# Sixteen small matmul tiles or thirty-two: the numerator product of a linear attention, cut by 32 channels in place of 64

## The reference

```
q, k, v = split(relu(x @ Wqkv.T))                     # 16 x 512 x 32 heads x 8
vk      = sum over tokens of [v, 1] (outer) k         # per head 9 x 8
num     = vk @ q                                      # per token and head 9 numbers
att     = num[:8] / (num[8] + 1e-15)
x       = layernorm(x + att @ Wp.T + bias)
h       = silu(x @ Wg.T) * (x @ Wu.T)                 # 768 hidden channels, weights int32 / 127
out     = layernorm(x + h @ Wd.T)
```

## Time and profile before

| | |
|---|---|
| median of three runs | 493.71 us |
| the profiled execution's own time | 493.46 us |
| its span, first to last instruction | 491.5 us |
| mean granted TensorE clock | 0.999 |
| TensorE matmuls busy | 485.7 us (99%) |
| VectorE busy | 417.6 us (85%) |
| ScalarE busy | 231.7 us (47%) |
| GpSimd busy | 87.5 us (18%) |

### The profile page before, as it was taken

How to read it: one execution, slowest core, us unless ns; L and a number is a source line. 1 busy time by engine, 2 the same in 40 slices (tenths; PEclk the granted TensorE clock), 3 DMA queues, 4 the chain that set the end, 5 groups by cost and what they waited for, 6 DMA issues and landing times.

```text
span 491.5 us, 11661 instructions
## 1 busy us (share of the span) xinstructions
PE 485.7 (99%) x4580; PEld 422.9 (86%) x4580; DVE 417.6 (85%) x963; ACT 231.7 (47%) x393; POOL 87.5 (18%) x70
## 2 busy tenths in 40 slices
PE   9999999999999999999999999999999999999996
PEld 5788888888889888898888988888898888989885
DVE  5878878888888888888979888888888888799896
ACT  4667435453453524536254354534535245255553
POOL 1320111311112121111311113111221211113012
PEclk9999999999999999999999999999999999999999
DMA  8325062271614527054270633617145260461212
GB/s 330 144 86 172 2 210 93 90 250 48 226 73 171 171 72 255 15 190 152 85 256 9 232 101 124 217 43 241 58 171 171 76 223 2 173 214 45 87 45 87
DMA packets 49512, 66.42 MB, mean 135 GB/s; under 512 B 3024, under 2 KB 33488, under 8 KB 49488
## 3 DMA queue, kind: packets, MB, share of 16 engines
q1 hardware_dynamic: 49344, 65.82, 38.8%
q10 hardware_dynamic: 144, 0.26, 0.1%
HBM read 35.66 MB, written 23.59 MB: 121 GB/s over the span
## 4 chain that ended last, share of the span: by engine, by line
PE 91%; DVE 6%; POOL 1%; issue 1%; ACT 0%; POOLq 0%; DVEq 0%
PE up_ps L997 33%; PE abcd_ps L997 25%; PE gate_ps L997 25%; PE abcd_ps L1049 4%; PE gate_ps L1027 2%; DVE h L573 1%; PE gate_ps L1168 1%; DVE h_lo L566 1%; DVE st L642 1%; POOL xb L325 1%; DVE r L659 1%; DVE attT_lo L566 0%; DVE att L702 0%; DVE mv L648 0%; ACT h_hi L379 0%
## 5 line engine op out<-in xcount | busy, mean ns | idle before, releaser
L302 POOL TENSOR_TENSOR rstd<-ve,minus_half 128x4 f32<-128x4 f32 (+2 forms) x36 | 43.9, 1219 | 317.0 <-DVE ve L654 316.9
L573 DVE SCALAR_TENSOR_TENSOR h<-up_ps,silu 128x512 f32<-128x512 f32 x95 | 65.3, 688 | 26.5 <-PE up_ps L997 15.5
L379 ACT ACTIVATE h_hi<-h 128x512 fp32r<-128x512 f32 (+1 forms) x97 | 60.6, 626 | 50.0 <-DVE h L573 49.4
L384 ACT ACTIVATE silu<-gate_ps 128x512 f32<-128x512 f32 x95 | 55.8, 587 | 53.6 <-PE gate_ps L997 53.5
L997 PE MATMUL gate_ps<-x1T_lo,wg_hi 128*128 128x512 f32 x192 | 74.9, 390 | 0.0
L997 PE MATMUL gate_ps<-x1T_hi,wg_hi 128*128 128x512 f32 x192 | 74.8, 390 | 0.0
L997 PE MATMUL up_ps<-x1T_hi,wu_hi 128*128 128x512 f32 x192 | 74.8, 389 | 0.0
L997 PE MATMUL up_ps<-x1T_lo,wu_hi 128*128 128x512 f32 x192 | 74.7, 389 | 0.0
L566 DVE TENSOR_TENSOR h_lo<-h,h_hi 128x512 fp32r<-128x512 f32 (+1 forms) x97 | 64.2, 676 | 0.5 <-ACT h_hi L379 0.2
L376 ACT ACTIVATE kv<-abcd_ps 128x512 f32<-128x512 f32 x55 | 32.9, 601 | 65.6 <-PE abcd_ps L997 65.6
L325 POOL TENSOR_TENSOR xb<-x_raw,bias_sb 128x1024 f32<-128x1024 f32 x16 | 38.7, 2421 | 73.2 <-DVE den L596 70.9
(11 more groups left out here) (181 smaller groups left out, 1061.8 us busy)
## 6 DMA issues: line engine op xcount, KB each, us to landing
x_raw<-x_tok SPq DMA_DIRECT2D x16, 512.0 KB, 5.7
att_way<-wg_raw SPq DMA_DIRECT2D x30, 256.0 KB, 2.9
wkv_raw<-att_way SPq DMA_DIRECT2D x30, 256.0 KB, 3.1
xT_raw<-x_chan SPq DMA_DIRECT2D x14, 512.0 KB, 6.1
x_way<-wu_raw SPq DMA_DIRECT2D x28, 256.0 KB, 2.1
wd_raw<-x_way SPq DMA_DIRECT2D x28, 256.0 KB, 3.0
out<-out_sb SPq DMA_DIRECT2D x14, 512.0 KB, 2.7
x<-r SPq DMA_DIRECT2D x13, 512.0 KB, 4.1
```

The costliest lines, as they stand in the source:

```text
L302: nc.gpsimd.tensor_tensor(rs[:, tiles], ve[:, tiles], minus_half[:, tiles], ALU.pow).then_inc(rs_ok, 1)
L379: nc.scalar.activation(dst, src, ACT.Copy).then_inc(ok, 1)
L384: nc.scalar.activation(silu[:, j % 2, :], gate_ps[bank_of(j)][:], ACT.Silu, scale=WSCALE).then_inc(silu_ok[j], 1)
L573: nc.vector.scalar_tensor_tensor(out=h[:, j, :], in0=up_ps[bank_of(j)][:], scalar=WSCALE, in1=silu[:, j % 2, :], op0=ALU.mult, op1=ALU.mul ...
```

## The change

`num` is cut by 32 channels in place of 64. A row tile then holds one group of 32 channels, so no zeros are needed: `vk` is written once (72 columns in place of 144), moving are 36 columns in place of 72, and there are 2 x 4 x 2 x 4 = 64 calls per block in place of 32. Four row tiles by two column tiles give eight tiles, and each of the four groups has a PSUM bank. The mask `own` shrinks, and is made by eight copies of 32 rows in place of four of 64. `den`, `rden` and `att` handle as many elements in as many instructions as before, in another order of dimensions.

```diff
-        own = sb("own", [P, 2, NW])
+        own = sb("own", [P, NW])
-        vk = sb("vk", [P, KC, 2, NW])
+        vk = sb("vk", [P, KC, NW])
-        num_ps = abcd[:, :, 0:NT * 2 * NW].rearrange("p m (t g n) -> p m t g n", t=NT, g=2)
+        num_ps = abcd[:, :, 0:NT * KC * NW].rearrange("p g (t k n) -> p g t k n", t=NT, k=KC)
...
-            for half in range(2):
-                rows = slice(half * HP, (half + 1) * HP)
-                nc.gpsimd.tensor_copy(own[rows, :, 0:GC], hblock[rows, rows].rearrange("p (g c) -> p g c", c=GC)).then_inc(own_ok, 1)
+            for g in range(NGC):
+                rows = slice(g * GC, (g + 1) * GC)
+                nc.gpsimd.tensor_copy(own[rows, 0:GC], hblock[rows, rows]).then_inc(own_ok, 1)
...
-                nc.vector.tensor_tensor(vk[:], vkv.unsqueeze(2).to_broadcast([P, KC, 2, NW]),
-                                        own[:].unsqueeze(1).to_broadcast([P, KC, 2, NW]), ALU.mult).then_inc(vk_ok, 1)
+                nc.vector.tensor_tensor(vk[:], vkv, own[:].unsqueeze(1).to_broadcast([P, KC, NW]), ALU.mult).then_inc(vk_ok, 1)
...
-            dve.wait_ge(own_ok, 4)
+            dve.wait_ge(own_ok, 2 * NGC)
...
                 for k in range(KC):
                     for t in range(NT):
-                        for half in range(2):
-                            rows = slice(half * HP, (half + 1) * HP)
-                            for o in (0, HP):
-                                last = mm(num_ps[o:o + HP, 2 * k + half, t, :, :].rearrange("p g n -> p (g n)"),
-                                          q[rows, k, t * P + o:t * P + o + HP], vk[rows, k, :, :].rearrange("p g n -> p (g n)"),
-                                          start=True, stop=True, tile_position=(half * HP, o))
+                        for o in (0, HP):
+                            for g in range(NGC):
+                                rows = slice(g * GC, (g + 1) * GC)
+                                last = mm(num_ps[o:o + HP, g, t, k, :], q[rows, k, t * P + o:t * P + o + HP], vk[rows, k, :],
+                                          start=True, stop=True, tile_position=(g * GC, o))
```

More of the change, by code:

```diff
@@ L86, in build @@
         kv = sb("kv", [P, NT, 2 * KC * NGC, VW])
-        vk = sb("vk", [P, KC, 2, NW])
-        den = sb("den", [P, 2 * KC, NT * 2 * GH])
-        rden = sb("rden", [P, 2 * KC, NT * 2 * GH])
+        vk = sb("vk", [P, KC, NW])
+        den = sb("den", [P, NGC, NT * KC * GH])
+        rden = sb("rden", [P, NGC, NT * KC * GH])
         att = sb("att", [P, NT, C])
@@ L331, in _ @@
             pool.wait_ge(consts_in, 16)
-            for half in range(2):
-                rows = slice(half * HP, (half + 1) * HP)
-                nc.gpsimd.tensor_copy(own[rows, :, 0:GC], hblock[rows, rows].rearrange("p (g c) -> p g c", c=GC)).then_inc(own_ok, 1)
[L335 to L338, removed]
+            for g in range(NGC):
+                rows = slice(g * GC, (g + 1) * GC)
+                nc.gpsimd.tensor_copy(own[rows, 0:GC], hblock[rows, rows]).then_inc(own_ok, 1)
+                pool.wait_ge(own_ok, 2 * g + 1)
+                nc.gpsimd.tensor_copy(own[rows, GC:NW], hcol[rows, g * GH:(g + 1) * GH]).then_inc(own_ok, 1)
+                pool.wait_ge(own_ok, 2 * g + 2)
             pool.wait_ge(bias_in, 16)
@@ L596, in rden_of @@
                 nc.vector.tensor_scalar(
-                    den[:].rearrange("p m (t g u) -> p m (t g) u", t=NT, g=2),
-                    num_ps[:, :, :, :, GC:NW].rearrange("p m t g u -> p m (t g) u"), DEN_EPS, None, ALU.add).then_inc(den_ok, 1)
+                    den[:].rearrange("p g (t k u) -> p g (t k) u", t=NT, k=KC),
+                    num_ps[:, :, :, :, GC:NW].rearrange("p g t k u -> p g (t k) u"), DEN_EPS, None, ALU.add).then_inc(den_ok, 1)
                 dve.wait_ge(den_ok, b + 1)
@@ L607, in att_of @@
                     for t in range(NT):
-                        for m in range(2 * KC):
+                        for g in range(NGC):
                             last = nc.vector.tensor_tensor(
[L610 to L614, removed]
+                                att[:, t, :].rearrange("p (k u e j) -> p j k u e", k=KC, j=NG, e=HD)[:, g],
+                                num_ps[:, g, t, :, 0:GC].rearrange("p k (u e) -> p k u e", e=HD),
+                                rden[:, g, t * KC * GH:(t + 1) * KC * GH].rearrange("p (k u) -> p k u", k=KC)
+                                .unsqueeze(3).to_broadcast([P, KC, GH, HD]), ALU.mult)
                     last.then_inc(att_ok, 1)
@@ L618, in att_of @@
                     last = nc.vector.tensor_tensor(
[L619 to L622, removed]
+                        att[:, t, :].rearrange("p (k g u e) -> p g k u e", k=KC, u=GH, e=HD),
+                        num_ps[:, :, t, :, 0:GC].rearrange("p g k (u e) -> p g k u e", e=HD),
+                        rden[:, :, t * KC * GH:(t + 1) * KC * GH].rearrange("p g (k u) -> p g k u", u=GH)
+                        .unsqueeze(4).to_broadcast([P, NGC, KC, GH, HD]),
                         ALU.mult)
```

## The result

The changed kernel takes **502.50 us** (median of six runs, 501.15 to 503.72) against 493.73: 1.0177 times as long, 95% interval 1.0161 to 1.0194. That is 8.8 us more. Slower was forecast, but at 2.9 us, and 502.5 lies outside the range that ended at 499.0. The profiled execution took 501.99 us, with a span of 499.8.

A forecast was written before the change was run, and what follows sets the result against it. TensorE was taken to bound the kernel, with all sixteen numerator stages on the path. Stage terms 0.31 + 0.90 + 0.13 = 1.34 us against 1.16, times 16, gave 493.7 + 2.9 = 496.6 us; range 490.8 to 499.0.

The forecast's parts named there:

- the rival that laid the break in `vk` to its second half `k`: Numerator stage has no break and starts pairs at 6 to 7 ns: 490.3 to 492.4 us; chance of faster 0.20.
- the first 33 pairs: Start of the numerator stage: 0.28 us as in `vk`, plus 0.03 for wider loads, 0.31 us.
- The other 95: Rest of the numerator stage's 128 pairs: 9.5 ns each, 0.90 us per block.
- near the measured row: Choice of 9.5 ns a numerator pair, after the 9.4 ns seen in the second half of the `vk` stage.
- the way to 10.8: Upper bound for numerator pairs: 33 in flight, each staying 356 ns with 64-column loads, 10.8 ns a pair, 5.0 us in all.
- The distance to `vk`: Time after the numerator's last matmul begins until the `vk` stage may start: 0.13 us.
- it is not the tile that has the overhead: Reading of the numerator and `vk` stages: a round of four tiles fell from 62.5 to 33 ns with the columns.
- the much faster rival: All eight numerator tiles at their own pace, starts 4 ns apart: stage 0.71 us, 7.2 us less, 486.5 us; chance 0.03.
- 16 x 0.18: Numerator stage 1.34 us against 1.16, 0.18 more in each of 16 blocks: 2.9 us in all.
- The rival of loads in turn: At most four 64-column loads run at once in the numerator: stage 1.78 us, 9.9 us more, 503.6 us; chance 0.06.
- W: Follow-up theory for the numerator stage: behind the break, pace is the pairs' time in flight over 32.

## Why the prediction was wrong

The mechanism of the stage was right: all sixteen stages on the path, 128 pairs whose pace after the first ones the supply of instructions holds down, a break at the 33rd pair (the rival that laid the break in `vk` to its second half `k` is out, since here the break comes ahead of that half), no cost of the mask, VectorE or GpSimd. Sizes: the first 33 pairs took 0.27 us (0.31 predicted). **The other 95** took 1.28 - 0.27 = 1.01 us, 10.6 ns each, where I took 9.5, "near the measured row": this term was mis-sized by 0.11 us. The row came from loads of 32 columns; the way to 10.8 for loads of 64 stood in the sum as the upper end. Its number was the better guess, in part by luck, since the theory that it comes from, a pair's time in flight, failed later on the floor and on the order by tiles. The distance to `vk` stayed 0.15 (0.13 predicted). Together 1.43 us against 1.34, 0.27 per block against 0.18, 4.3 us in all against 2.9. That alone is inside the range that the forecast had for itself.

One reading was wrong. The prediction put the fall of a round from 62.5 to 33 ns down to the columns, "as half the columns should be". But between those two stages the loads change as well, from 64 columns to 32, and tile by tile, with 36 columns moving and loads of 64, a pair still takes 58 ns. So most of the fall came from the loads, "it is not the tile that has the overhead" doesn't hold, and eight tiles of this shape could give a pair per 58 / 8 = 7.3 ns, an estimate, not the 4 ns of the much faster rival. The forecast did not hang on it, since the supply's 8.3 ns is slower still, but the margin is small.

**The step that failed** is the sum "16 x 0.18": it took every block alike and had no term for the way in which the instructions come to TensorE. It counted the instructions of the stage, and asked how quickly TensorE starts them; their coming was put at nothing without a reason. Where code runs for the first time, the quick instructions can be used up before the next packet of 256 has come, and TensorE stands still, three times, 3.4 us in this execution. With the 0.3 us of the head this is the way from 4.3 to 8.0 of the 8.8 us. The other 0.8 I can't place: 0.3 lies in the span, and the rest in what the medians have over the profiled spans. That these gaps are waits for instructions is shown by the loop written out (20 us more with the change, nothing without it), by the move of `vk`, which took the two late ones away, and by the packets, which come at each gap.

The rival of loads in turn named 503.6 us, close to the 502.5 measured. That is chance: it had a stage of 1.78 us, and the stage took 1.43.

What sets the floor of 8.3 ns a pair is narrowed to the supply of instructions (nearly the same for eight and sixteen tiles, the same for loads of 32 with 36 columns and of 16 with 18, and slower than the first 32 pairs start). Why a load wider than 32 adds to it stays open: W's arithmetic gave 1.33 us for loads of 48 (1.32 measured), but W failed on the floor and on the order by tiles. With loads of 64 the tiles' 7.3 ns lie so near the floor that each may hold the other up; no run here shows it. Which link of the supply sets the 8.3 ns is not shown.

## What to carry to other kernels

Cutting a small matmul stage into more tiles pays only while the instructions keep up: compare the time that the tiles need for a pair with the time in which pairs have been seen to start in a long stage, here 8.3 ns, and not with the pace of the first few. A row is a price only for its own shape: if the load is wider than in the row, take the bound that allows for it. And count instructions in a row against the instruction queue's packets, above all in code that runs once: a loop hides that price from its second turn on, straight code can pay it anew in each turn.

## What the hardware showed that was not expected

- Instructions come in packets of 16 KB, 256 of TensorE's. The kernel before, with 256 quick ones ahead of slow matmuls in each turn, never waited, in the loop or written out; the changed kernel's 384 waited in nine of fourteen stretches when written out, 0.2 to 2.3 us at a time. Its first numerator stage waited too, with 256 in a row soon behind 128 others.
- A gap of TensorE can cost more than itself. In the written-out changed kernel TensorE stood still for 2.26 us, and the `vk` stage behind it ran at a mean granted clock of 0.73, so partly at 1.2 GHz: it took 0.99 us from first to last in place of 0.77. From this numerator stage to the next (221.88 to 256.01 us) passed 34.1 us, 4.0 more than in turns without a gap. In another turn the granted clock was 0.50 behind the gap. It did not fall behind every gap: in the loop, behind 1.60 us, it stayed at 1.00, and the gap cost 1.8 us. Columns of the windows: us, busy of PE, PEld, DVE, ACT, POOL, granted clock, DMA share, GB/s.

```profile
225.77 0.99 PE L1024 MATMUL gate_ps<-kv 128*32 128x36 f32 x64
...
223.40:225.66 2.26, 0.00 (x1) 0.00 (x0) 0.00 (x0) 0.00 (x0) 0.00 (x0) 1.00 0.43 121
225.66:226.70 1.04, 1.04 (x66) 0.85 (x65) 0.79 (x2) 0.00 (x0) 0.30 (x1) 0.73 0.02 6
...
96.70:97.60 0.90, 0.90 (x53) 0.84 (x52) 0.50 (x2) 0.00 (x0) 0.63 (x1) 0.50 0.04 11
```
